# Products between transposes in 32-column tiles, in a four-layer transformer kernel

## What is computed

```python
m = silu(mod) @ ada_w + ada_b
h = layer_norm(x) * (1 + scale_msa) + shift_msa
q, k, v = split(h @ qkv_w + qkv_b, 3)
x = x + (mha(q, k, v) @ self_o_w + self_o_b) * gate_msa
q = layer_norm(x, g, b) @ q_w + q_b
k, v = split(context @ kv_w + kv_b, 2)
x = x + (mha(q, k, v) @ cross_o_w + cross_o_b)
h = layer_norm(x) * (1 + scale_mlp) + shift_mlp
x = x + (gelu(h @ mlp_w1 + mlp_b1) @ mlp_w2 + mlp_b2) * gate_mlp
```

## Time and profile before

| | us |
|---|---|
| median of 3 runs | 2457.98 |
| lowest, highest | 2456.62, 2459.28 |
| the profiled execution, its own time | 2459.47 |
| its span, first to last instruction | 2457.7 |

### The profile page before, as it was taken

The page is one execution under the profiler, slowest core; times in us unless marked ns, Lnnn a source line. Parts: engine busy times, 40 slices in busy tenths (PEclk is TensorE's granted clock), DMA queues, the critical chain, the costliest instruction groups (busy, mean ns, idle before and its releaser), DMA issues.

```text
span 2457.7 us, 93436 instructions
## 1 busy us (share of the span) xinstructions
PE 2394.8 (97%) x41326; PEld 1616.7 (66%) x41326; DVE 1875.6 (76%) x3532; ACT 1263.5 (51%) x1810; POOL 466.9 (19%) x510
## 2 busy tenths in 40 slices
PE   6889999999999999999999999999999999999998
PEld 3556666666666666666666666666666666666666
DVE  5777788888888888887777777778777777777763
ACT  1444555555555555554554554555555545545544
POOL 0112211211121211111111111212212212212121
PEclk8989999999999999999999999999999999999999
DMA  6431222222222222222221221222231322312211
GB/s 214 133 113 61 99 86 78 78 88 85 80 84 84 91 93 76 93 89 72 70 88 60 85 78 55 88 88 70 94 108 60 106 70 76 100 60 89 85 40 39
DMA packets 143669, 209.27 MB, mean 85 GB/s; under 512 B 14978, under 2 KB 75588, under 8 KB 143268
## 3 DMA queue, kind: packets, MB, share of 16 engines
q1 hardware_dynamic: 143268, 203.30, 24.2%
HBM read 58.34 MB, written 4.39 MB: 26 GB/s over the span
## 4 chain that ended last, share of the span: by engine, by line
PE 91%; DVE 5%; issue 1%; ACT 1%; DMA 1%; SPq 0%; POOL 0%; POOLq 0%; DVEq 0%; ACTq 0%
PE ring L1220 38%; PE ring L1216 13%; PE o_acc L1380 12%; PE score L1327 11%; PE score L1349 9%; PE ring L1174 4%; PE score L1354 3%; DVE row_max_F L1008 3%; DVE row_max_G L1008 2%; ACT probs L1147 1%; DMA gate_now_P<-gate_rows 0%; SPq L693 0%; PE ring L1256 0%; DMA q_F<-q_parts 0%; DMA k_G<-k_parts 0%
## 5 line engine op out<-in xcount | busy, mean ns | idle before, releaser
L1147 ACT ACTIVATE probs<-score 120x2048 f32<-120x2048 f32 (+1 forms) x320 | 601.6, 1880 | 302.2 <-PE score L1354 273.5
L1008 DVE TENSOR_REDUCE row_max_F<-score 128x8 f32<-128x2048 f32 x192 | 438.6, 2285 | 88.8 <-PE score L1327 86.2
L1158 ACT ACTIVATE h_t<-ring,cols 128x256 f32<-128x256 f32 x384 | 160.6, 470 | 415.5 <-PE ring L1220 289.3
L1008 DVE TENSOR_REDUCE row_max_G<-score 128x16 f32<-128x1920 f32 x128 | 276.2, 2158 | 65.4 <-PE score L1327 65.4
L1220 PE MATMUL ring<-x_t_E,w_fc 128*32 128x256 f32 x4736 | 279.6, 380 | 0.0
L1030 DVE STREAM_TRANSPOSE o_turned<-o_acc 128x512 f32<-128x512 f32 x224 | 159.4, 712 | 127.7 <-PE o_acc L1380 127.2
L1220 PE MATMUL ring<-w_fc,h_t 128*32 128x256 f32 x3680 | 215.4, 380 | 0.0
L1220 PEld LDWEIGHTS ring<-x_t_E,w_fc 128*32 128x32 f32 x4736 | 149.0, 110 | 100.2
L1380 PE MATMUL o_acc<-probs,v_self 128*17 128x256 f32 x3072 | 203.8, 383 | 0.4 <-DVE o_turned L1030 0.4
L817 POOL TENSOR_TENSOR x<-x,gated 128x512 f32<-128x512 f32 x48 | 61.2, 1274 | 612.1 <-DVE gated L1049 611.8
L1349 PE MATMUL score<-q_F,k_F 32*128 32x256 f32 x3072 | 166.1, 302 | 9.0 <-ACT probs L1147 4.5
(11 more groups left out here) (154 smaller groups left out, 4155.7 us busy)
## 6 DMA issues: line engine op xcount, KB each, us to landing
k_F<-k_parts SPq DMA_DIRECT2D x192, 256.0 KB, 2.5
q_G<-q_parts SPq DMA_DIRECT2D x128, 256.0 KB, 2.6
k_G<-k_parts SPq DMA_DIRECT2D x256, 120.0 KB, 2.1
q_F<-q_parts SPq DMA_DIRECT2D x96, 256.0 KB, 3.4
gate_now_P<-gate_rows SPq DMA_DIRECT2D x48, 256.0 KB, 3.9
gate_now_E<-gate_rows SPq DMA_DIRECT2D x48, 256.0 KB, 3.7
x<-in_x_dram SPq DMA_DIRECT2D x16, 256.0 KB, 4.0
out_dram<-x SPq DMA_DIRECT2D x16, 256.0 KB, 2.4
```

The costliest lines, as they stand in the source:

```text
L1008: nc.vector.tensor_reduce(dst, src, AX.X, ALU.max).then_inc(row_max_ready[r].sem, 1)
L1147: nc.scalar.activation(probs[v % 2][0:keys, :, :], score[0:keys, :].rearrange("p (h q) -> p h q", h=2 * GROUPS), ACT.Exp, scale=SCALE).the ...
L1158: last = nc.scalar.activation(h_t[:, c, :], ps[:, c % 2 * NT:(c % 2 + 1) * NT], ACT.Gelu_apprx_tanh, bias=col(m, "fc1", c))
```

## The change

`in_column_tiles` no longer looks at intervals: it gives every step that is not a transpose the flag true. Every product then runs in 32-column tiles. No step moves to another place, and no wait, buffer or transfer is added or removed. Fifteen lines fewer stand ahead of all else, so line L1205 of the changed kernel is L1220 of the one before, and L1159 is L1174.

```diff
 def in_column_tiles(steps):
 
-    tiled, at = [], 0
-    while at < len(steps):
-        end = at
-        while end < len(steps) and scores(steps[end][2]) == scores(steps[at][2]):
-            end += 1
-        fixed = [step not in TURNED for r, m, step, n, here in steps[at:end]
-                 if step in TURNED or step in IN_COLUMNS or step[:2] == "PV"]
-        now = fixed[0] if fixed else True
-        for r, m, step, n, here in steps[at:end]:
-            if step in TURNED:
-                now = False
-            elif step in IN_COLUMNS or step[:2] == "PV":
-                now = True
-            tiled.append(now)
-        at = end
-    return tiled
+    return [step not in TURNED for r, m, step, n, here in steps]
```

## The result

| | us, median | ratio to before, 95% interval |
|---|---|---|
| before | 2457.76 | |
| after | 2475.68 | 1.0069 [1.0057, 1.0081] |
| after, run again (e9) | 2477.64 (before: 2458.06) | 1.0076 [1.0063, 1.0090] |

The change makes the kernel 18 to 20 us slower: +17.9 the first time (by the interval +14.0 to +19.9), +19.6 the second. The forecast was +19.6, 2477.6.

What follows compares the result with a forecast made beforehand. TensorE was taken to bound the kernel. Changed seams add 25.6 us, waits absorb 6.2, leaving 19.4; with the ends, +19.6 on the median 2457.98 gives 2477.6 us, range 2469 to 2485.

Steps and rivals of the forecast that it cites:

- C to T: Seam on TensorE from a column-tiled product or `PV` to transposes: 0.11 us more than to another column-tiled group.
- T behind C: Four transposes following a column-tiled product or `PV` take 0.05 us more than behind a whole product.
- T to C: Seam on TensorE from transposes to a column-tiled product: 0.10 us more than to a whole product.
- the set behind T: A column-tiled product that follows transposes: itself taken as 0.02 us slower.
- Rival 2: Going from transposes to a column-tiled product costs no more than to a whole one: 2470.1 us, chance 0.08.
- rival 3: Going from a column-tiled product to transposes is cheap, so the change is faster: about 2455 us, chance 0.02.
- H2 P.LN and H0 R.C: Intervals with a product, then transposes, before a waiting score block: the wait absorbs all of the added 0.09 us each.
- rival 1: Waits absorb little because VectorE's reductions come late too: 2483.8 us, or 2489.8 with slower products behind transposes; chance 0.07.
- M, PR, C: Intervals with a product between two transposes: 0.285 us more TensorE work each, of which a 0.084 wait is absorbed.
- T P R: 18 intervals with transposes, a product, then a score block: nearly nothing, -0.02 us each, as a costly exit seam goes.
- Rival 4: Waits that don't show hide more of the added TensorE work: within 5 us of before, chance 0.04.
- Rival 5: Each of 5,340 added matmuls costs its issue: +288 us, 2746, or +133 by the skill's 60 cycles; chance 0.01.

Runs made afterwards that it cites:

- e9: The changed kernel run again, unaltered, in five rounds: 2477.64 us against 2458.06 for the kernel before, ratio 1.0076.
- e2: Kernel before with only 40 products, ahead of score blocks that wait for VectorE's reduction, in column tiles: 2456.78 us against 2458.33, ratio 0.9994.
- the control: Kernel before built again with the same instructions and order, only other line numbers: 2459.09 us against 2458.06, ratio 1.0002.
- e3: Kernel before with only 25 products between two transposes, with no wait behind, in column tiles: 2463.13 us against 2458.33, ratio 1.0022.
- e4: Kernel before with products whole in all intervals that hold neither transposes nor `PV`, 276 steps more: 2464.83 us against 2458.33, ratio 1.0026.

## Why the prediction was right

- **What bounds the kernel.** TensorE, as read. VectorE's and ScalarE's busy times stayed the same to 0.1 us while the time followed TensorE's seams.
- **The seams.** C to T 0.11, T behind C 0.05, T to C 0.10, the set behind T 0.02: each was measured as forecast, to 0.01. T to C was the thin one, with three clean cases before; after, 72 cases stand at 0.20 between the last transpose and the product's first matmul where T to P has 0.11, and the set behind takes what it takes behind a score block. Rival 2 falls, as does rival 3: 181 seams from a product to transposes cost the same as those from `PV`.
- **Absorption.** The intervals H2 P.LN and H0 R.C took the addition fully, in the changed kernel and alone in e2; rival 1 falls. In M, PR, C each interval kept 0.184 of 0.285, I had 0.201: these transposes have 120 columns, and they and their seam are a little shorter than the ones I took. The forms cost 0.280 there for the 0.285 of the forecast, and the wait had been 0.097 (0.293 from the last transpose to the block where 0.196 is the least), not 0.084.
- **The sum.** The table's 182 intervals were forecast at 18.35 and gave 17.9, most of the difference in M, PR, C. The other 14 were forecast at 1.05 and gave 2.6 and 3.8, but one of them alone has 1.8 and 3.0. It starts at 149 us, and from 151 to 154 us TensorE was granted 0.50, the lower of its two clocks (1.2 GHz), in the changed kernel. In the kernel before the clock is 1.00 there, and 0.50 from 159 to 163 us. The interval at that place, which has no product, is 2.35 shorter in the changed kernel. The prediction has no term for such things; with them, all 639 intervals give 19.1 and 19.8 against the control, for 19.4. So each kind was right by its mechanism, and that the total agrees to 0.4, and the second pair of medians to 0.1, is in part luck.
- **Ends.** The last products of the kernel gave +0.14 for +0.15; nine products stand behind its one transpose step, not ten, which changes nothing in the sum. The first score block starts 1.8 and 1.4 earlier in the two traces of the changed kernel than in the control. Kernels of equal code up to there (e2, e3) are 1.1 apart, so neither my +0.05 nor a small gain can be shown.
- **One step was wrong and cost nothing.** The 18 T P R intervals were taken at -0.02 because a whole product seemed to pay dearly ahead of a score block. e4 shows that it pays nothing there. Each such interval really costs +0.135 on TensorE (0.09 at T to C, 0.04 for the slower set behind, nothing at the exit), but it is one with a wait behind it, the very wait that I had read as a seam, and it takes all of it in: +0.01 us in 15.
- **Rivals 4 and 5.** Rival 4 (within 5 us of before) falls with the result, +14.0 at the least. Rival 5 falls with e2 and e3. The 60 cycles for each matmul that the Trainium skill gives ("TensorEngine Tiling (Array Packing)", Instruction Overhead) show nowhere as an addition when 32-column tiles take the place of a whole matmul: a set with its seam to the next takes 1.727 us and so does a whole step.

The rule of the Trainium skill that a change of tiling mode drains TensorE ("TensorEngine Tiling (Array Packing)", Key Properties) is borne out and can be given a size here: 0.09 to 0.11 us and slower first instructions, for 32, 64 and 128 columns in any pair that ran, with products, `PV` and transposes. Out of a row-tiled score block it shows only in the slower first instructions; the seam itself is 0.20 to any shape.

## What to carry to other kernels

Whole and column-tiled products stream equally fast (1.73 us for either here), so choose a product's form by its neighbours on TensorE: the tile shape of what stands ahead and behind, transposes being whole. Each change of shape costs some 0.12 to 0.20 us (least from transposes to a column set, most from `PV` to a whole product), and only where TensorE doesn't stand for another engine right behind; look for the distance from the releaser's end to the next start, which is 0.05 to 0.06 where it waits. And before a distance between two groups is booked as the price of a seam, check that no releaser ends just ahead of it.

## What the runs showed of the hardware

- The matmuls of a column set start in fours: 0, 7, 13 and 20 ns, and the next four at 216 (464 sets of the kernel before, medians). A whole step starts its single ones at 0, 216, 432 and so on, and 64-column tiles start in twos. So the tiles run beside one another at the pace of one whole matmul. That is why four times the records cost nothing, and the 0.054 of rival 5 is only an average.
- The price of a seam doesn't depend on which shapes meet: 32 to 64, 64 to 128 and 32 to 128 columns all put 0.31 us between the start of the last matmul of one group and that of the first of the next (read from the starts in nanoseconds, hundreds of seams), against 0.20 from 32 to 32 and 0.22 from whole to whole. That is behind products and `PV`, with their 256 moving columns; behind transposes, with 128, it is 0.20 against 0.11.
- A group's own start is slower behind another shape, and for products the more so the wider the tiles: 0.02 for a set of 32-column tiles, 0.05 for 64, 0.10 whole (1.62 against 1.51 from first to last matmul). For four transposes it is 0.06. For a whole product that came as no surprise; that 64 columns lie between was new.
- Behind row-tiled score blocks every shape starts after 0.20. Ahead of them products of every form and `PV` leave 0.31, and transposes 0.20. So there the form matters only through the entry's 0.02 to 0.10.
